# Cross-attention with a nine-expert feed-forward: expert tiles that begin after two of four groups are routed, and weight halves split during attention

## The reference

```python
x = x + tanh(g0) * attention(ctx, layernorm(x))        # 16 batches of 128 tokens, 8 heads of 16
# feed-forward: 9 experts, the best two for each token
scores = sigmoid(layernorm(x) @ gate.T + bias)         # 2048 x 9
top_scores, selected = top_k(scores, 2); top_scores /= sum(top_scores)
for e in range(9):
    h = silu(x_flat @ w1[e].T) * (x_flat @ w3[e].T)    # x_flat: the normalised x, 128 -> 352
    out += cw[:, e:e+1] * (h @ w2[e].T)                # 352 -> 128
x = x + tanh(g1) * out
```

## Time and profile before

| | |
|---|---|
| three executions, us | 271.84, 271.94, 274.58 |
| median, us | 271.94 |
| the profiled execution: time, us | 274.52 |
| its span, us | 272.7 |
| busy share of the span: PE, PEld, DVE, ACT, POOL | 70%, 58%, 64%, 49%, 43% |
| mean granted TensorE clock, of full | 0.868 |
| DMA moved | 21.02 MB |

### The profile page before, as it was taken

One profiled execution on the slowest core, in us unless ns is written; L12 is line 12 of the kernel. 1 busy time (PEld: TensorE's weight loads), 2 busy tenths in 40 slices (PEclk: granted clock), 3 DMA queues, 4 the chain that ended last, 5 costly groups with the idle time before them and its releaser, 6 DMA issues.

```text
span 272.7 us, 5842 instructions
## 1 busy us (share of the span) xinstructions
PE 189.9 (70%) x1480; PEld 158.4 (58%) x1481; DVE 175.5 (64%) x681; ACT 133.8 (49%) x383; POOL 116.7 (43%) x196
## 2 busy tenths in 40 slices
PE   0399988989887878766300005999999999999300
PEld 0377745666555645453200004999999999998200
DVE  2248875787998779677685911566776677676125
ACT  1355539888867667573570101355455445544000
POOL 3315741332314651761377700156555655555400
PEclk9999999999999799975555555799999999999955
DMA  5904400094000010180012203022222222220096
GB/s 186 303 20 123 110 0 2 5 324 161 4 1 21 30 33 0 39 287 16 5 54 79 88 20 79 2 54 61 60 62 64 59 52 64 65 56 33 0 257 204
DMA packets 23718, 21.02 MB, mean 77 GB/s; under 512 B 3520, under 2 KB 19844, under 8 KB 23696
## 3 DMA queue, kind: packets, MB, share of 16 engines
q1 hardware_dynamic: 19152, 15.67, 19.8%
q0 software_dynamic: 2432, 4.30, 4.9%
q10 hardware_dynamic: 2112, 0.80, 1.2%
HBM read 14.81 MB, written 6.47 MB: 78 GB/s over the span
## 4 chain that ended last, share of the span: by engine, by line
PE 50%; DVE 21%; issue 9%; DMA 8%; SPq 6%; POOL 3%; ACT 2%; another core or an unknown queue 0%; DVEq 0%; POOLq 0%; ACTq 0%
PE ps_b L1007 10%; PE score_ps L975 5%; PE score_ps L976 5%; PE score_ps L977 5%; DVE mx L672 5%; PE score_ps L831 3%; PE pt_ps L1017 3%; DMA mask_b<-in_mask 3%; PE ps_b L940 3%; PE score_ps L841 3%; DMA w<-y_rows 3%; PE ps_a L919 2%; POOL x_rows L490 2%; PE ps_a L990 2%; DVE st L737 2%
## 5 line engine op out<-in xcount | busy, mean ns | idle before, releaser
L505 POOL DMA_INDIRECT y_rows<-probsT,ids x40 | 39.7, 992 | 11.1 <-POOL ids L503 11.1
L333 ACT ACTIVATE probs<-score_ps,less 128x128 f32<-128x128 f32 x128 | 37.1, 394 | 2.4 <-DVE less L676 2.4
L490 POOL DMA_INDIRECT x_rows<-stage,slot x32 | 33.5, 1047 | 9.8 <-issue 8.6
L1007 PE MATMUL ps_b<-w,probsT 128*128 (+1 forms) x240 | 33.4, 275 | 1.1 <-DVE probsT L808 1.1
L420 ACT COPY probsT<-pt_ps 128x256 f32<-128x256 f32 x40 | 14.9, 372 | 37.1 <-PE pt_ps L1017 31.6
L1007 PEld LDWEIGHTS ps_b<-w,probsT 128*128 128x128 f32 (+1 forms) x240 | 31.6, 190 | 1.7 <-issue 1.6
L484 POOL TENSOR_TENSOR rs<-ve,minus_half 128x1 f32<-128x1 f32 x16 | 9.0, 564 | 53.2 <-DVE ve L742 41.2
L793 DVE TENSOR_TENSOR probs<-probs,score_ps 128x352 f32<-128x352 f32 x40 | 20.9, 522 | 16.9 <-issue 11.5
L975 PE MATMUL score_ps<-w_high,xg_low 128*128 x80 | 30.5, 382 | 0.0
L990 PE MATMUL ps_a<-cst,xg 128*128 128x128 f32 x40 | 11.6, 289 | 26.7 <-DMA xg<-x_rows 25.9
L976 PE MATMUL score_ps<-w_low,xg_high 128*128 x80 | 26.6, 333 | 0.0
(11 more groups left out here) (149 smaller groups left out, 463.4 us busy)
## 6 DMA issues: line engine op xcount, KB each, us to landing
w<-in_w13T SPq DMA_DIRECT2D x3, 1056.0 KB, 8.4
xg<-x_rows SPq DMA_DIRECT2D x40, 65.0 KB
ctx_r<-in_ctxT SPq DMA_DIRECT2D x4, 512.0 KB, 5.0
w<-y_rows SPq DMA_DIRECT2D x8, 256.0 KB, 6.3
w<-in_w2T SPq DMA_DIRECT2D x1, 1728.0 KB
mask_b<-in_mask SPq DMA_DIRECT2D x4, 256.0 KB, 6.2
out<-xs SPq DMA_DIRECT2D x4, 256.0 KB, 3.3
xs<-in_x SPq DMA_DIRECT2D x3, 256.0 KB, 8.8
```

What stands on the lines that cost most here:

```text
L333: last = nc.scalar.activation(probs[:, r % 2, h, :], score_ps[:, r % 2, h, :], ACT.Exp, bias=less[:, r % 2, h:h + 1], scale=SCALE)
L490: pool.indirect_dma_start(x_rows[:, :], bass.IndirectOffsetOnAxis(ap=slot[:, c, p:p + 1], axis=0), stage[:, c, p, :], None, bounds_check=l ...
L505: pool.indirect_dma_start(y_rows[:, :], bass.IndirectOffsetOnAxis(ap=ids[:, r:r + 1], axis=0), yt[:, r, :], None, bounds_check=last_row, o ...
L1007: last = nc.tensor.matmul(bank[7][:, 0:D], hidT[0:cn, q3, c, :], w2[0:cn, bass.ds(e3, 1), c, :].rearrange("p o d -> p (o d)"), start=(c == ...
```

## The change

The expert tiles are cut into three parts, 8, 8 and 24 tiles (`TILES`). `table(n)` makes each part's rows: the first two parts hold only full tiles of 128 rows from the rows that are placed so far, the last one the rest. The attention loop now has 17 steps; what is left of it (the last two batches' norm, projection and logits, and the whole routing of group 3) stands in functions `between(k)` after the first ten tile steps of each engine. `x_rows` is filled with padding as a whole (19584 rows of 520 bytes, 10.2 MB) by one DMA of SP before attention, in place of nine blocks at the end. The weights are loaded before attention begins and straight into `w13_low`; in steps 0 to 8 ACT rounds one expert's 704 columns to `w13_high` and POOL subtracts in place. A hidden row is turned in three pieces of 128 (two overlap, with zero rows in w2) and copied by ACT alone. `y_rows` is laid out by token, so that a partition's reads are contiguous, and the last pieces are smaller. The second norm reads x in place and writes `stage` directly.

```diff
+EARLY = (TR, TR)
+TILES = EARLY + (NT - sum(EARLY),)
+PARTS = [slice(0, 4), slice(4, 8), slice(8, 12), slice(12, 14), slice(14, 16)]
@@ sync
+            for n in range(NE // 3):
+                sp.dma_start(w13_low[:, 3 * n:3 * n + 3].bitcast(F32), ...).then_inc(ld_w13[n], 16)
+            sp.wait_ge(pad_set, 2)
+            sp.dma_start(x_rows[0:NE * CAP]..., pads[:]...to_broadcast([P, CAP // P, NE * RW])).then_inc(st_pad, 16)
             sp.wait_ge(scores, 2 * UN + 1)
-            for n in range(NE // 3):
-                sp.dma_start(w13[:, 3 * n:3 * n + 3], ...).then_inc(ld_w13[n], 16)
+            for n in range(len(EARLY)):
+                sp.wait_ge(rows_known, n + 1)
+                for p in range(UN):
+                    sp.wait_ge(st_rows[p], (NG - len(EARLY) + n) * 32)
+                for r in range(TR):
+                    if n >= 1:
+                        sp.wait_ge(st_y[r], n * 16)
+                    row = sp.value_load(row_of[0:1, n * TR + r:n * TR + r + 1], ...)
+                    sp.dma_start(xg[:, r, :], x_rows[bass.ds(row, P), :]).then_inc(ld_tile[r], 16)
@@ scalar, step(k)
+                if k < NE:
+                    act.wait_ge(ld_w13[k // 3], 16)
+                    nc.scalar.copy(w13_high[:, k], w13_low[:, k].bitcast(F32)).then_inc(w_high, 1)
-                if isinstance(k, int) and k in (NB + 1, NB + 3, NB + 4):
-                    ...
-                        nc.scalar.copy(w13_high[:, e], w13[:, e]).then_inc(w_high, 1)
+            def between(k):
+                ...
+                if k == 4:
+                    sigmoid_exps(NG - 1)
+                    nc.scalar.preload_act_table(ACT.Silu)
@@ gpsimd, step(k)
+                if on(k, 3):
+                    rstd2_of(k - 3)
+                if k < NE:
+                    split(k)
+            def split(e):
+                pool.wait_ge(w_high, e + 1)
+                nc.gpsimd.tensor_tensor(w13_low[:, e], w13_low[:, e].bitcast(F32), w13_high[:, e].bitcast(F32), ALU.subtract).then_inc(w_low, 1)
+            rstd2_of(NB - 2)
+            scatter(NG - 2, (0, 1))
+            rstd2_of(NB - 1)
+            scatter(NG - 2, (2, 3))
             for k in range(NT):
                 tile(k, k % TR)
+                if 2 <= k < 2 + UN:
+                    scatter(NG - 1, (k - 2,))
@@ vector
-            lows(range(1, NE))
+                if k == NB:
+                    table(0)
+            def between(k):
+                ...
+                if k == 3:
+                    table(1)
+                if k == 4:
+                    logit(NB - 1)
+                    clamp(NG - 1)
+                if k == 5:
+                    make_keys(NG - 1)
+                if k == 6:
+                    choose(NG - 1)
+                if k == 7:
+                    weigh(NG - 1)
+                if k == 8:
+                    dve.wait_ge(ranked, NG)
+                    ...
+                    place_rows(NG - 1)
+                    label_rows(NG - 1)
+                if k == 9:
+                    table(2)
```

More of the change, by code:

```diff
@@ L263, in _ @@
+            sp.wait_ge(rows_known, len(TILES))
             for p in range(UN):
-                sp.wait_ge(st_rows[p], NG * 32 + 16)
-            for r in range(TR):
-                sp.dma_start(xg[:, r, :], x_rows[bass.ds(rows[r], P), :]).then_inc(ld_tile[r], 16)
-            with sp.Fori(1, NT // TR) as i:
+                sp.wait_ge(st_rows[p], NG * 32)
+            with sp.Fori(len(EARLY), NT // TR) as i:
                 for r in range(TR):
@@ new lines, in step, with keep, sigmoid_exps @@
+                if routed(k, r, 6) is not None:
+                    sigmoid_exps(routed(k, r, 6))
+            def keep(b):
+                act.wait_ge(ln2, b + 1)
+                par, place = b // UN % 2, b % UN
+                nc.scalar.copy(stage[:, par, 1, place, 0:D], stage[:, par, 0, place, 0:D]).then_inc(kept, 1)
+            def sigmoid_exps(g):
+                act.wait_ge(lg_ready, g + 1)
+                if g >= 1:
+                    act.wait_ge(weighed, g)
+                nc.scalar.activation(sigs[:], logits[:], ACT.Exp, scale=-1.0).then_inc(sig_exp, 1)
@@ L401, in tile, with turned_back @@
+            def turned_back(k):
+                act.wait_ge(ul_turned, k - 1)
+                if k >= 4:
+                    act.wait_ge(o_mm, min(k - 3, NB))
+                low, high = 0 if on(k, 2) else 1, 2 if on(k, 3) else 1
+                nc.scalar.copy(ulT[:, k % 2, low:high, :], ps_b[:, low * P:high * P].rearrange("p (a t) -> p a t", a=high - low)).then_inc(ul_copied, 1)
+            turns(step)
             def tile(k, r, i):
@@ L496, in _ @@
             last_slot = pool.to_reg(NE * CAP - 1)
-            turns(pool, step)
+            turns(step)
             last_row = pool.to_reg(2 * NB * P - 1)
@@ L578, in _ @@
             route_links = {}
-            LINKS = {"clamp": 1, "keys": 4, "choose": 4, "weigh": 5, "place": 3}
+            LINKS = {"clamp": 1, "keys": 4, "choose": 4, "weigh": 4, "place": 3}
             def route_link(g, stage_name, ins):
@@ L781, in tile @@
+            dve.wait_ge(ld_gate, 2 * 16)
+            turns(step)
+            unturn(NB - 1, 1, NG - 2)
+            weigh(NG - 2)
+            place_rows(NG - 2)
+            label_rows(NG - 2)
             def tile(k, r, i):
@@ new lines, in rank @@
+            def rank(g):
+                pe.wait_ge(chosen, g + 1)
+                sel, at = both[:].rearrange("p b e -> p (b e)"), 3 * P + NE
+                nc.tensor.matmul(ps_b[:, at:at + GZ], rows_below[:], sel, start=True, stop=False, skip_group_check=True)
+                for n in range(1, UN):
+                    nc.tensor.matmul(ps_b[:, at + n * NE:at + GZ], ones[:], sel[:, 0:(UN - n) * NE], start=False, stop=(n == UN - 1), skip_group_check=True)
+                for b in range(UN):
+                    last = nc.tensor.matmul(ps_b[:, at + GZ:at + GZ + NE], ones[:], both[:, b, :], start=(b == 0), stop=(b == UN - 1), skip_group_check=True)
+                last.then_inc(ranked, 1)
@@ L949, in _ @@
             pe.wait_ge(ld_gate, 2 * 16)
-            turns(pe, step)
+            turns(step)
+            turn_out(NB - 1, NG - 2)
             pe.wait_ge(table_set, 1)
```

498 lines of the change are left out of this document (244 added, 254 removed).

## The result

The changed kernel took 282.98 us (median of 4, 282.52 to 284.54); the kernel before took 272.49 beside it (median of 4). The ratio is 1.038, with a 95% interval of 1.031 to 1.045: slower. In every profiled run here the time is its span plus 1.8 to 1.9 us (282.85 for a span of 281.0). The two spans therefore show 8.3 of the 10.5 us. The ratios in this document leave out executions over 1.5% above the fastest of their kernel (one of e3's eight took 466.19 us, one of a2's four 288.56); the medians hold all of them.

A forecast was written before the change was run, and what follows sets the result against it. A loop of waits bound attention, where no engine was full; PE bound the tile phase. 272.7 + 14.3 - 31.1 + 22.0 + 1.5 - 2.6 = 276.8 us of span, so 276.0 in time; range 265 to 284.

The forecast's parts named there:

- A: Attention: the weight split on ACT and POOL lengthens the steps, +14.3 us (+8 to +18).
- B: Hand-over from attention to tile 0: the first table starts at once, without padding in the way, -31.1 us.
- the ring: Attention: closed loop of waits from xn through ACT's rounding and POOL's subtraction to the next xn, 7.1 us a step.
- s: Attention: length of POOL's 704-column subtraction, taken as 1.73 us, bounds 0.81 and 2.1.
- C: First 14 tile steps: work moved in from attention and routing delays them, +22.0 us (+16 to +26).
- step 14 = 38.9 + 11.7 + 0.9: Tile phase: tile 11 at 38.9, three tiles 3.9 apart, 0.9 for SP's slower register work; step 14 starts at 51.5 us.
- D: Tile steps 10 to 14 and after: PE's clock may fall to 1.2 GHz, 0 to +3, taken as +1.5 us.
- E: End: read back in larger packets, smaller last additions and store, -2.6 us (-1.5 to -4).
- the ring does not bind: Attention: only ACT's rounding costs, about +1.5 us in all, time 263.2 us; chance 0.13.
- the clock falls inside the ring: Attention: PE at 1.2 GHz makes a step about 8 us, +0.9 for six to eight steps, 282; chance 0.13.
- the second block is short: Tile phase: the last group's slots come at 24 us, the delay there is +15, time 269.0 us; chance 0.17.
- the padding is late: Attention step 10: under 140 GB/s POOL waits for padding, at 100 GB/s some 35 us, time 310; chance 0.03.

The follow-up runs named there:

- e3: The changed kernel with POOL's nine subtractions left out and ACT's roundings kept; 264.25 us, ratio 1.004 to the kernel before.
- a2: The changed kernel itself run again, on chip 7, nothing altered; 285.34 us, ratio 1.0432 to the kernel before.
- e1b: The changed kernel with POOL's subtraction one step later, on chip 7; 276.42 us, ratio 1.013 to the kernel before.
- e4: The changed kernel with the subtraction one step later and the last group's row DMAs behind outputs 5 to 8; 272.01 us, ratio 0.9975.
- e1: The changed kernel with POOL's subtraction one step later, on chip 6; 265.97 us, ratio 1.0091 to the kernel before.
- e6: e4 with ACT rounding in steps 7 to 15 and DVE, not POOL, subtracting in steps 8 to 16; 263.77 us, ratio 0.969.
- e9: e6 with the second and third tables cut in three, and weights and padding issued only after the first attention scores; 264.74 us, ratio 0.9682.
- e5: The kernel before with only the new end, token rows side by side and read back in five parts; 262.23 us, ratio 0.997.
- e2: The changed kernel with the last group's row DMAs behind POOL's outputs 5 to 8, not 2 to 5; 269.90 us, ratio 1.0212.

## Why the prediction was right, and by how much it missed

The direction was right, and the time, 283.0, lies inside the range of 265 to 284 at its slow end. The size was not: +4.1 us were forecast and +10.5 measured, and "slower by one to three per cent" was 3.8% (3.1 to 4.5). The range reaches from 2.5% faster to 4.4% slower, so lying inside it says little; the terms and the rows say more. The time is 7.0 us above the 276.0 forecast. 4.2 of them are in the terms, where the misses of A and B, +1.3 and -1.3, cancel by luck. The other 2.8 come from taking the median 0.8 below the profiled span, as before had it. That profiled run of before was 2.6 us above its median; that of the changed kernel was not, and its median is 2.0 above the span.

- **A, the ring: right in mechanism and size.** 7.21 us a step against 7.1, s 1.67 against 1.73 (and against the 1.55 that the prediction works out from the Trainium skill). Opening the ring wins 7.0 us on chip 7 (e1b), 8.8 on chip 5 (e4) and 10.6 on chip 6 (e1), or 6.8, 7.9 and 9.3 counted from the first `v_cur`; the rest goes only when the split leaves POOL and these steps (e6). The first xn comes 4.0 later where 3.0 were forecast, since the loads that the text called covered cost 1.4 us ahead of attention, which e9 takes back. The steps behind the ring give 2.1 back, for 1.8.
- **B: right.** -32.4 against -31.1. e5 shows that its size is the chip's as well: where SP pads in 5.04 us, tile 0 comes 32.1 us after the last variance in the kernel before and not 38.6, and B is about -26 (e2 against e5).
- **C: right in its places, 3.0 too small.** The slots at 31.1, the third output before the stop, tile 11 at 39.4 (forecast 38.9) and tiles 12 and 13 at 4.1 apart are as worked out. The slots' 31.1 is in part luck: the stalls as listed put step 8 at 25.7 and leave it 5.1 us, while tile 8 was turned at 27.3 and the slots followed 3.8 later. The mis-sized term is "step 14 = 38.9 + 11.7 + 0.9": three tiles took 15.2 us and not 12.6. The 6.97 us to tile 14 hold the late starts of ACT and DVE. On chip 6, which shows none of them, e1 with the same order of work has 48.9 us to tile 14, under the forecast's 51.5, and tiles 12 to 14 are 3.9 to 4.2 apart. The 0.9 for SP's work beside POOL is not shown. Of the table loads of ACT, the one at 169.26 begins as the instruction before it ends and the next one starts at 170.56: 1.28 us, and nothing of the 1.38 of draining that the prediction cites from the Trainium skill.
- **D: right in number, half in cause.** +2.0 against +1.5. The clock is in 0.9 of it: tile 15 comes 2.99 us behind tile 14 in place of 2.07, with the granted clock at 0.76 from 204 to 208 us. 0.7 are in the other steps, five of which take 2.2 us, and 0.4 lie between the last tile's turn and its output. No run shows the forecast's 3.5 us for a tile.
- **E: too large.** -1.9 by the trace, -0.7 as measured alone. The read back itself went from 6.91 to 4.10 us in the chain, but DVE's ten additions, 0.70 or 0.43 each, then stand one behind the other: 6.2 us.
- **Rival "the ring does not bind" was priced wrongly.** It took 1 to 2 us for rounding and a subtraction outside the ring, and had the kernel at 263.2, faster than before. e1b is that case, and it takes 276.4, slower than before by 1.3%. 7 us of the difference are in attention, where A is +8.5 and not +1.5. The missing cost is POOL's subtraction holding DVE's small operations; the rest is in C, D and the 2.8 us between median and span.
- **Rival "the clock falls inside the ring" came true and costs 0.1 us a step.** Of two ring steps of the changed kernel (stretches of 7 us; the clock is the third number from the end) the one has full clock and the other half:

```profile
76.00:83.00 7.00, 5.14 (x48) 3.46 (x46) 3.80 (x16) 5.73 (x17) 2.52 (x5) 0.99 0.01 2
83.00:90.00 7.00, 6.07 (x37) 4.12 (x38) 4.19 (x14) 3.59 (x12) 2.39 (x3) 0.51 0.00 1
```

  xn to xn is 7.15 in the first and 7.28 in the second. PE has slack in the ring, so 0.9 us a step was too much.
- **Rival "the second block is short"** did not happen: the slots came at 31.1 and not at 24. **Rival "the padding is late"** neither: it was through at 70 us, as forecast, and POOL had no wait for it. The bound of 140 GB/s counts the padding alone; with the weights, 13.4 MB from 27 to 102 us, it is 179.

## What to carry to other kernels

Before moving work to an engine that looks idle, write out its list for one step and ask what small operation stands behind the new one and who waits for that: before the change POOL was busy a third of each step (1.58 us of 4.7), and a rounding of 0.77 with a subtraction of 1.67 us in the wrong place cost six steps 2.3 us each. The same nine roundings and subtractions cost 17.6 us on ACT and POOL in steps that wait in a ring, and 1.4 to 1.9 on ACT and DVE in later steps where DVE waits anyway. Look also at what a long operation on POOL does to small ones on DVE that run beside it. And a wait cut out of one stage is worth what the next stage leaves of it: the scatter moved behind three more outputs freed tiles 13 to 15 on chip 6, and the next load that needed its rows took part of the gain back.

## What the hardware showed that was not expected

On some chips ACT and DVE begin late while POOL issues indirect DMAs one behind the other. The eight profiles on chips 5 and 7 and the first one of the changed kernel have 7 to 11 waits marked "remote" each, 12 to 23 us in all; the longest is 6.54 us. During four in five of them (70 of 87) POOL issues such a DMA. The first profile of the kernel before has two, 3.05 us in all. The four kernels on chip 6 have none, though e1 and e3 issue the same DMAs in the same places. That the DMAs delay the engines is argued from this, not shown: no run leaves them out. SP's register work differs between these traces too. One line's answer for SP's loads in the changed kernel (ns: least, median, most):

```profile
L264 SPq FUSED_REGOPS  x16: 3/42/457, 147.3 to 200.9; - x16
```

and in e1 on chip 6:

```profile
L264 SPq FUSED_REGOPS  x16: 42/42/48, 135.7 to 186.2; - x16
```

What differs between the chips isn't shown. It is worth 10 us to the kernel before (263.2 against 273.1), about as much as the change that was studied: compare two kernels on one chip only.
